# The gram of a chunk as two bursts of 64-row matmuls in the two halves of TensorE's rows

## The reference, cut to what matters

```python
e = stack([tbl_f[ids[:, f]] for f in range(64)], axis=1)      # 512 x 64 x 16
x_vec = e
for W, b in ((W0, b0), (W1, b1), (W2, b2)):
    z = einsum('bhd,bfd->bhfd', x_vec, e)                     # h: 64, then 128, 128
    x_vec = einsum('oc,bcd->bod', W, z.reshape(512, h * 64, 16)) + b[None, :, None]
    outs.append(x_vec.sum(axis=2))
h = concatenate([concatenate(outs, axis=1), dense_ctx], axis=1)
y = relu(relu(h @ W_top1 + b_top1) @ W_top2 + b_top2) @ W_top3
```

## Time and profile before

| | us |
|---|---|
| time before, median of 3 runs | 1192.84 |
| lowest and highest of them | 1191.19, 1193.23 |
| the profiled execution's own time | 1193.48 |
| its span, first to last instruction | 1191.7 |

### The profile page before, as it was taken

One profiled execution on the slowest core, in us unless ns is written; L12 is line 12 of the kernel. 1 busy time (PEld: TensorE's weight loads), 2 busy tenths in 40 slices (PEclk: granted clock), 3 DMA queues, 4 the chain that ended last, 5 costly groups with the idle time before them and its releaser, 6 DMA issues.

```text
span 1191.7 us, 13969 instructions
## 1 busy us (share of the span) xinstructions
PE 1120.7 (94%) x4212; PEld 758.3 (64%) x4212; DVE 1011.0 (85%) x685; ACT 704.5 (59%) x682; POOL 989.1 (83%) x419
## 2 busy tenths in 40 slices
PE   0379999999999999999999999999999999999998
PEld 0146666666666666666766666666666666667685
DVE  4478998989989999989898998999898889897542
ACT  2245566566666666675666666656666666665533
POOL 6669999999999999999999999999999997776000
PEclk9989999999999999999999999999999999999999
DMA  6552232525252515334252524252342525242991
GB/s 226 137 161 65 85 83 78 161 65 166 73 150 63 155 46 147 91 88 150 64 165 73 156 78 133 68 144 71 111 127 76 154 73 160 76 151 106 273 297 48
DMA packets 103835, 142.85 MB, mean 120 GB/s; under 512 B 11745, under 2 KB 55009, under 8 KB 103042
## 3 DMA queue, kind: packets, MB, share of 16 engines
q1 hardware_dynamic: 95618, 140.42, 39.1%
q0 software_dynamic: 8192, 2.11, 2.0%
HBM read 114.96 MB, written 27.53 MB: 120 GB/s over the span
## 4 chain that ended last, share of the span: by engine, by line
POOL 62%; PE 17%; issue 14%; DMA 4%; DVE 1%; SPq 1%; ACT 1%; POOLq 0%; ACTq 0%; DVEq 0%
POOL z_lo L509 46%; POOL emb L500 16%; PE acc L1015 9%; PE acc L1010 3%; DMA z<-gram_scratch 3%; PE turn_gram_ps L1079 1%; DMA land<-x_scratch 1%; PE z_ps L1141 1%; ACT z_hi L977 0%; DVE z_lo L754 0%; DVE z L577 0%; SPq L441 0%; SPq L369 0%; PE x0t_ps L1183 0%; PE turn_gram_ps L1183 0%
## 5 line engine op out<-in xcount | busy, mean ns | idle before, releaser
L509 POOL TENSOR_TENSOR z_lo<-z,z_hi 128x2048 fp32r<-128x2048 f32 x159 | 734.9, 4622 | 47.0 <-ACT z_hi L789 44.1
L1015 PE MATMUL acc<-z_hi,w_hi 128*128 128x512 f32 x960 | 412.4, 430 | 3.0 <-POOL z_lo L509 2.1
L789 ACT ACTIVATE z_hi<-z 128x2048 fp32r<-128x2048 f32 x160 | 306.3, 1914 | 181.4 <-PE acc L1015 170.4
L1015 PE MATMUL acc<-z_hi,w_lo 128*128 128x512 f32 x960 | 378.8, 395 | 0.0
L1015 PE MATMUL acc<-z_lo,w_hi 128*128 128x512 f32 x960 | 378.8, 395 | 0.0
L577 DVE TENSOR_TENSOR z<-operand_even,x_shift 128x2048 f32<-128x2048 f32 x144 | 328.5, 2282 | 31.8 <-DMA x_shift<-x_scratch 16.8
L500 POOL DMA_INDIRECT emb<-in_tables,rows_chunk x256 | 254.0, 992 | 62.0 <-issue 56.9
L1010 PE MATMUL acc<-z,w_sb 128*128 128x512 f32 x640 | 293.7, 602 | 0.6 <-ACT x L818 0.4
L589 DVE TENSOR_TENSOR z_lo<-z_ps,z_hi 128x1024 fp32r<-128x1024 f32 x160 | 194.5, 1215 | 71.0 <-ACT z_hi L798 71.0
L1015 PEld LDWEIGHTS acc<-z_hi,w_hi 128*128 128x128 f32 x960 | 180.8, 188 | 62.8 <-issue 18.9
L577 DVE TENSOR_TENSOR z<-operand_odd,x_shift 128x2048 f32<-128x2048 f32 x96 | 218.8, 2279 | 0.5 <-ACT operand_odd L765 0.3
(11 more groups left out here) (92 smaller groups left out, 454.2 us busy)
## 6 DMA issues: line engine op xcount, KB each, us to landing
land<-x_scratch SPq DMA_DIRECT2D x128, 256.0 KB
land<-x_scratch SPq DMA_DIRECT2D x128, 128.0 KB
x_shift<-x_scratch SPq DMA_DIRECT2D x16, 1024.0 KB, 5.8
gram_scratch<-gram SPq DMA_DIRECT2D x32, 512.0 KB, 4.3
x_shift<-x_scratch SPq DMA_DIRECT2D x16, 768.0 KB, 7.7
z<-gram_scratch SPq DMA_DIRECT2D x10, 1024.0 KB, 10.8
x_scratch<-emb SPq DMA_DIRECT2D x32, 192.0 KB, 2.9
x_shift<-gram_scratch SPq DMA_DIRECT2D x6, 1024.0 KB, 10.5
```

What stands on the lines that cost most here:

```text
L509: pool.tensor_tensor(z_lo[:, slot], z[:, Z_SLOT[pos]], z_hi[:, slot].bitcast(F32), ALU.subtract).then_inc(subtracted, 1)
L789: act.activation(z_hi[:, SPLIT_SLOT[pos]], z[:, Z_SLOT[pos]], ACT.Copy).then_inc(rounded, 1)
L1015: mm = pe.matmul(acc[:, :], w[:, tile, :], zz[:, slot, q, :], start=False, stop=stop and n == 2)
```

## The change

`form_blocks` makes the block matrices of all four blocks in one instruction of 4 x 4 x 64 = 1,024 columns. The mask now repeats after 64 partitions, so each half of the partitions holds the block matrix of its own four samples. `gram_of(c, half)` replaces four calls by two: for two blocks each it issues four matmuls of 64 rows x 128 weight columns x 256 moving columns, in turn in the lower and the upper half of PE's rows. The lower half's go to `turn_gram_ps`, the upper half's to the bank of `x0t_ps`, which the turned x0 had held until `form_blocks` read it. ACT empties both banks after each burst (`take_gram(c, half, bank)`), with the same number of columns as before. PE's wait before it overwrites acc2's last unit is now for `gram_staged`, since `turn_x0` writes into the bank that the gram uses.

```diff
+HALF_ROWS = P // 2
+TILE_B = HALF_ROWS // EMBED
+HALVES, BANK_BLOCKS = 2, BLOCKS // 2
+GRAM_BANKS = 2
-        mask_sb = sb("mask_sb", [P, GROUP_B])
+        mask_sb = sb("mask_sb", [P, TILE_B])
-        blocks = sb("blocks", [P, 2, GROUP_B, FIELDS])
+        blocks = sb("blocks", [P, BLOCKS, TILE_B, FIELDS])
+        gram_banks = [turn_gram_ps[:, :], x0t_ps[:, :, :].rearrange("p b f -> p (b f)")]
...
-            def form_block(c, b):
-
-                if b == 0:
-                    dve.wait_ge(x0_turned, c.count(1, 1))
-                if not (c.is_(0) and b < 2):
-                    dve.wait_ge(gram_done, c.count(BLOCKS, b - 1))
+            def form_blocks(c):
+
+                dve.wait_ge(x0_turned, c.count(1, 1))
+                if not c.is_(0):
+                    dve.wait_ge(gram_done, c.count(HALVES))
+                shape = [P, BLOCKS, TILE_B, FIELDS]
                 dve.tensor_tensor(
-                    blocks[:, b % 2], x0t_ps[:, b:b + 1, :].to_broadcast([P, GROUP_B, FIELDS]),
-                    mask_sb[:, :].rearrange("p (b f) -> p b f", f=1).to_broadcast([P, GROUP_B, FIELDS]),
+                    blocks[:, :, :, :],
+                    x0t_ps[:, 0:BLOCKS, :].rearrange("p (k o) f -> p k o f", o=1).to_broadcast(shape),
+                    mask_sb[:, :].rearrange("p (k b f) -> p k b f", k=1, f=1).to_broadcast(shape),
                     ALU.mult).then_inc(block_ready, 1)
...
-            def take_gram(c, b):
+            def take_gram(c, half, bank):
+                act.wait_ge(gram_done, c.count(HALVES, half + 1))
+                if bank == 0 and not (c.is_(0) and half == 0):
+                    act.wait_ge(gram_stored, c.count(32, 16 * half))
...
-                            pe.wait_ge(block_ready, c.count(BLOCKS))
+                            pe.wait_ge(gram_staged, c.count(BLOCKS))
...
+            def gram_of(c, half):
+                if half == 0:
                     pe.wait_ge(x2t_ready, c.count(1, 1))
+                    pe.wait_ge(block_ready, c.count(1, 1))
                 else:
+                    pe.wait_ge(gram_staged, c.count(BLOCKS, GRAM_BANKS))
+                for k in range(BANK_BLOCKS):
+                    b = half * BANK_BLOCKS + k
+                    for r in range(GRAM_BANKS):
+                        rows = slice(r * HALF_ROWS, (r + 1) * HALF_ROWS)
+                        mm = pe.matmul(gram_banks[r][:, k * TILE_B * FIELDS:(k + 1) * TILE_B * FIELDS],
+                                       x2t[rows, b * P:(b + 1) * P],
+                                       blocks[rows, b].rearrange("p b f -> p (b f)"), start=True, stop=True)
+                mm.then_inc(gram_done, 1)
...
                 layer2(c, 2, (0,))
                 gram_of(prev, 1)
                 layer2(c, 2, (1, 2, 3))
-                layer2(c, 3, (0,))
-                gram_of(prev, 2)
-                layer2(c, 3, (1, 2, 3))
+                layer2(c, 3, range(QUAD))
                 turn_x0(c)
-                gram_of(prev, 3)
```

More of the change, by code:

```diff
@@ L661, in round_ @@
                 layer2_middle(c, 1)
-                form_block(prev, 0)
+                form_blocks(prev)
                 layer1(nxt, 1)
@@ L730, in _ @@
             layer2(end, 3, 0)
-            form_block(prev, 3)
             layer2_middle(end, 3)
             split_half(layer2_group(end, 3), 1)
-            form_block(end, 0)
-            form_block(end, 1)
+            form_blocks(end)
             sum2(end)
@@ L822, in take_x2t @@
                 if not c.is_(0):
-                    act.wait_ge(gram_done, c.count(BLOCKS))
+                    act.wait_ge(gram_done, c.count(HALVES))
                 act.activation(x2t[:, :], turn_gram_ps[:, :], ACT.Copy).then_inc(x2t_ready, 1)
-            def take_gram(c, b):
[L827 to L831, removed]
+            def take_gram(c, half, bank):
+                act.wait_ge(gram_done, c.count(HALVES, half + 1))
+                if bank == 0 and not (c.is_(0) and half == 0):
+                    act.wait_ge(gram_stored, c.count(32, 16 * half))
+                act.activation(gram[:, :, :].rearrange("p f (k r b) -> p r k b f", k=BANK_BLOCKS, r=GRAM_BANKS)[:, bank],
+                               gram_banks[bank].rearrange("p (k b f) -> p k b f", k=BANK_BLOCKS, f=FIELDS),
+                               ACT.Copy).then_inc(gram_staged, 1)
             def round_(c, look_up=True):
@@ L860, in round_ @@
                 round_half(m, 0)
-                take_gram(prev, 0)
+                take_gram(prev, 0, 0)
                 round_unit(m, 3)
+                take_gram(prev, 0, 1)
                 to_bank(d, 0, 0, released_by_layer1(m, 0))
@@ L871, in round_ @@
                 take_x1(nxt)
-                take_gram(prev, 1)
+                take_gram(prev, 1, 0)
                 round_half(d, 1)
@@ L879, in round_ @@
                 round_unit(e, 3)
[L880 removed]
+                take_gram(prev, 1, 1)
                 round_half(e, 1)
@@ L950, in _ @@
                 if i == 2:
-                    take_gram(prev, 0)
+                    take_gram(prev, 0, 0)
                 round_unit(g, 3)
-                if i == 0:
-                    take_gram(end.plus(-2), 3)
+                if i == 2:
+                    take_gram(prev, 0, 1)
                 if i == 3:
-                    take_gram(prev, 1)
+                    take_gram(prev, 1, 0)
                 round_half(g, 1)
@@ L980, in _ @@
             take_x2t(end)
-            take_gram(end, 0)
+            take_gram(end, 0, 0)
             round_w2(2)
-            take_gram(end, 1)
+            take_gram(end, 0, 1)
             round_w2(3)
             round_gram(2)
-            take_gram(end, 2)
+            take_gram(end, 1, 0)
             round_gram(3)
-            take_gram(end, 3)
+            take_gram(end, 1, 1)
             for k in range(4, GRAM_BLOCKS):
@@ L1071, in turn_x2 @@
                 t.then_inc(x2_turned, 1)
-            def gram_of(c, b):
-                if b == 0:
+            def gram_of(c, half):
+                if half == 0:
                     pe.wait_ge(x2t_ready, c.count(1, 1))
+                    pe.wait_ge(block_ready, c.count(1, 1))
                 else:
-                    pe.wait_ge(gram_staged, c.count(BLOCKS, b))
-                pe.wait_ge(block_ready, c.count(BLOCKS, b + 1))
-                pe.matmul(turn_gram_ps[:, :], x2t[:, b * P:(b + 1) * P],
-                          blocks[:, b % 2].rearrange("p b f -> p (b f)"), start=True, stop=True).then_inc(gram_done, 1)
+                    pe.wait_ge(gram_staged, c.count(BLOCKS, GRAM_BANKS))
[7 more added lines that the diff above has]
+                mm.then_inc(gram_done, 1)
             def round_(c, last=False):
@@ L1160, in _ @@
             top1_begin(2)
-            gram_of(end, 1)
             top1_begin(3)
             layer3(0)
-            gram_of(end, 2)
+            gram_of(end, 1)
             layer3(1)
-            gram_of(end, 3)
             pe.wait_ge(sum2_ready, CHUNKS)
```

15 lines of the change are left out of this document (2 added, 13 removed).

## The result

The changed kernel takes 1200.48 us (median of 5 runs, 1198.33 to 1203.6), the kernel before 1192.71 (5 runs, 1191.19 to 1193.23). The ratio is 1.0067, interval [1.0047, 1.0086]: 0.7% slower, against a forecast of 1201.8. The profiled execution took 1201.17 us, its span 1199.4, 7.7 more than before.

What follows compares the result with a forecast made beforehand. POOL, at 65.15 us a round, was taken to bound the steady part, with a nearly slackless loop through gathers, block and gram. Loop +10.2 and last part -0.6 gave +9.6, 9 taken: 1201.8 us, range 1191 to 1213.

Steps and rivals of the forecast that it cites:

- What bounds: Steady rounds: POOL has no slack, 65.15 us a round; a loop through gathers, block and gram has 0.73 us usable slack.
- the link that I had read: End of ACT's rounding of the last group's position 1 to POOL's subtraction: 0.23 to 1.55 us, mean 0.81, 0.73 usable.
- The block, +0.54: DVE's single 1,024-column block instruction takes 1.23 us instead of 0.68, so the first gram waits 0.54 us longer.
- The burst, 1.08: Four 64-row matmuls on PE take 1.08 us, between bounds of 0.86 and 1.72, against 0.86 for a gram.
- side by side in full: Rival: a burst takes 0.86 us, the loop loses 0.41 a round, 4.9 in 12; +3.5 us, 1196.3; chance 0.20.
- Going over, 0.2 and 0.2: PE pays 0.2 us going to 64 rows and 0.2 back around each burst, unless it was waiting anyway.
- The sum on the loop: First gram +0.96, second +0.62, together 1.58 us less 0.73 slack: 0.85 a round, 10.2 us over 12 rounds.
- The last part, -0.6: From 1003.8 us to PE's last chunk at 1104: dropped grams against bursts, net -0.6 us.
- The total: 10.2 - 0.6 = +9.6 us, of which 9 taken: 1202.5 profiled, 1201.8 median.
- the signs that were named: POOL's waits over 10 us, rounds about 66, PE waiting for the block nearly every round, block 1.23, burst 1.1.

Runs made afterwards that it cites:

- the run with the useless instruction: The kernel before with one unused 1,024-element VectorE reduction ahead of a chunk's first block: 1205.32 us, ratio 1.0089.
- whole rows: The changed kernel with one 128-row matmul instead of each pair of 64-row matmuls, half of the gram left out: 1195.45 us, ratio 1.0019.
- the block stood early: Block formed ahead of VectorE's half subtraction that hangs on the landed tile: changed kernel 1191.25 us, kernel before (first block only) 1191.33 us.
- the run with the halves apart: The changed kernel with both lower-half matmuls of a burst written ahead of both upper-half ones: 1201.43 us, ratio 1.0071.
- the run on one half: The changed kernel with both matmuls of every pair on rows 0 to 63: 1237.29 us, ratio 1.0356.
- the lighter POOL in the changed kernel: The changed kernel as timed, with a quarter of one POOL subtraction per round given to VectorE: 1201.5 us, ratio 1.0064.
- the fastest kernel of this study: The changed kernel with block early, bursts behind position 1, and a quarter of one POOL subtraction per round given to VectorE: 1181.63 us, ratio 0.9903.
- the kernel before with a lighter POOL: The kernel before with its first block early and a quarter of one POOL subtraction per round given to VectorE: 1185.47 us, ratio 0.9937.

## Why the prediction was right

**What bounds.** POOL's work before, and a loop with some of its slack left: right. The experiments that move the loop or POOL's work and leave the other alone follow it. The slack was read at one link only, though, and is smaller at another (0.59 against 0.73, the run with the useless instruction). In the changed kernel POOL is at its floor of 0.08 at the link that I had read, while that other link stays open (0.24 at least, 0.46 in the mean); that the second block instruction no longer stands ahead of it is a likely reason, not a tested one.

**The block, +0.54.** Measured +0.53: from the start of the landed half's rounding to the block's end it is 4.65 us, before 4.12.

**The burst, 1.08.** This term was mis-sized, and no run shows it: it was my choice between the bounds of 0.86 and 1.72. A burst takes 0.86 us and 0.01 to 0.04 of offset; each matmul is two instructions, and those of the other half start beside them. The rival "side by side in full" had the right burst.

**Going over, 0.2 and 0.2.** Measured 0.2 and 0.16; whole rows took 0.65 for two bursts off the path, where one "in" is covered. What PE does in that time, which the expectations call draining, no run shows; only its length was measured.

**The sum on the loop.** Less what is above 0.08 of slack, the path from block to POOL was 31.73 and is 32.45. With the block that is 0.72 + 0.53 = 1.25 us instead of 1.58; the difference is nearly all the two bursts' 0.36. Less 0.73 it gives 0.52 a round, 6.2 us in 12; the trace has 6.3 in its twelve rounds, and 0.5 more between chunk 2's gathers and the first of them. So 10.2 was 3.4 too much for the 6.8 of the whole stretch. The rival of full overlap has the mechanism in every part but came out at 4.9 for the loop: besides 0.11 a round that its terms fell short of the measured 1.25, it too subtracts a mean slack, while the transfers from gather to block vary (19.7 to 21.3 us in the changed kernel and 19.1 to 20.9 before, in the mean 0.07 more than the block explains), and a round with more slack than it needs pays nothing back to another.

**The last part, -0.6.** Measured -0.95, with one step missed: PE's wait for ACT's copy of x2, 0.5 to 0.6 us each (5.7 in 11 waits), which the fourth gram behind the transposes had covered. I named the gram's going as pure relief. With bursts of 0.86 and without this wait it would have been -1.5.

**The total.** +9.6 was forecast for the profiled execution, +7.7 came, of which 1.3 lie ahead of the grams. The time fits better than the terms do, and that part is luck: 3.4 too much in the loop stand against 1.3 of the start and 0.6 in the end, which were no part of the reasoning. Of the signs that were named, POOL's waits came to 9.1 us and not to over 10, the rounds to 65.72 where about 66 was written, PE waits for the block in every round, and the block takes 1.21; the burst of 1.1 did not come, it is 0.86.

## What to carry to other kernels

Work saved on an engine that does not set the pace is worth nothing until that one is relieved: the same bursts, with the longer block instruction that comes with them, cost 7.8 us here, gave nothing measurable once the block stood early (1191.25 against 1191.33 us), and gained 3.8 us when POOL was lighter. When several instructions become one, look at who waits for the first of them: the sum got shorter (one block of 1.21 for four of 0.68) and the latency that counted longer. And ask of every instruction that goes what it was covering.

## What the runs showed of the hardware

- PE starts f32 matmuls of the two row halves 0.01 to 0.04 us apart (947.57 and 947.58, 947.86 and 947.90 in the changed kernel). In the run with the halves apart the upper half's first instruction starts at 947.46, ahead of three of the lower half's that come first in the program, the earliest of them at 947.74.
- Going from 128 rows to 64 and back costs 0.2 and 0.16 us (1.06 for a burst of 0.86, and 8.56 for 8.40, in the changed kernel), where a matmul of 256 f32 columns takes 0.43, two instructions of 0.216.
- In the run on one half an idle stretch of PE of 1.48 us was followed by 7 us at a granted clock of 0.51. In that run the clock fell to 0.5 in 7 rounds of 13, for some 3.4 us in the other six; in the runs with the halves apart, with whole rows and with the lighter POOL in the changed kernel it did so in one round each, behind waits of 1.95, 2.09 and 2.15 us for the block; and in the changed kernel, with such waits of up to 2.08, in none.
- The small subtraction given to VectorE takes 0.71 us when POOL issues gathers beside it, and 3.02 when it starts within a subtraction of POOL, whose end (439.88 + 3.51 = 443.39) it outlasts by 0.56:

```profile
439.88 3.51 POOL L516 TENSOR_TENSOR z_lo<-z,z_hi 128x1536 fp32r<-128x1536 f32 x1
...
440.93 3.02 DVE L605 TENSOR_TENSOR z_lo<-z,z_hi 128x512 fp32r<-128x512 f32 x1
```

```profile
443.70 0.71 DVE L600 TENSOR_TENSOR z_lo<-z,z_hi 128x512 fp32r<-128x512 f32 x1
```

The first is the fastest kernel of this study, the second the kernel before with a lighter POOL; the medians of the 15 such instructions are 2.99 and 0.68 us. Why the one takes longer was not tested. The rounds of the fastest kernel are the 64.4 us that PE's own work gives, so no loss from these 2.3 us shows; whether a better place for the instruction gives more was not tried.
